# Base, expert and router weights in one product, lora a step later, and scores in two row tiles

## What is computed

```python
x = x + attn(cond(x))        # cond: a 32x32 mix of positions per sequence, with a bias
#   attn: q, k, v = x @ Wq, x @ Wk, x @ Wv; 32 query heads of 16, 8 kv heads, rope on q and k
#         scores = q k^T / 4, causal mask, softmax, times v, then @ Wo
x = x + ffn(cond2(x))        # cond2: a 9-tap grouped convolution along the 512, plus a context
#   ffn:  base_out = z @ base_W.T + base_b
#         probs = softmax(z @ router_W.T + router_b)      # 15 router outputs
#         w = the 8 largest probs, gathered per expert    # 8 experts
#         h = z @ A.T                                     # 8 experts x rank 16 = 128
#         lora = (h * w) @ B * 2
#         return base_out + lora
```

## Time and profile before

| | us |
|---|---|
| median of 3 runs | 747.89 (747.72 to 748.15) |
| the profiled execution | 748.08 |
| its span, first to last instruction | 746.1 |
| PE busy | 711.7 (95%) |
| DVE busy | 543.9 (73%) |
| ACT busy | 272.5 (37%) |
| POOL busy | 147.6 (20%) |
| chain that ended last: PE | 82% of the span |
| chain: ACT, POOL, DVE | 7%, 5%, 3% |
| granted TensorE clock, mean | 0.990 |

### The profile page before, as it was taken

The page is one execution under the profiler, slowest core; times in us unless marked ns, Lnnn a source line. Parts: engine busy times, 40 slices in busy tenths (PEclk is TensorE's granted clock), DMA queues, the critical chain, the costliest instruction groups (busy, mean ns, idle before and its releaser), DMA issues.

```text
span 746.1 us, 13077 instructions
## 1 busy us (share of the span) xinstructions
PE 711.7 (95%) x4478; PEld 628.5 (84%) x4510; DVE 543.9 (73%) x1424; ACT 272.5 (37%) x635; POOL 147.6 (20%) x116
## 2 busy tenths in 40 slices
PE   5879999999999999999999999999999999999985
PEld 4578888888888888888888888888889888888874
DVE  5457787777778777777877777788777777877763
ACT  4135433333443333344333323433333344333331
POOL 5232201222221122222102222210122222012211
PEclk9979999999999999999999999999999999999999
DMA  7751100111110011111100111110011111001000
GB/s 189 169 242 29 43 17 27 42 42 42 42 42 31 15 38 42 42 42 42 40 16 28 42 42 42 42 42 14 28 42 42 42 42 42 19 23 42 29 29 29
DMA packets 27392, 35.43 MB, mean 47 GB/s; under 512 B 11651, under 2 KB 13347, under 8 KB 26998
## 3 DMA queue, kind: packets, MB, share of 16 engines
q1 hardware_dynamic: 26374, 34.88, 15.1%
q10 hardware_dynamic: 864, 0.14, 0.1%
q0 software_dynamic: 144, 0.28, 0.1%
HBM read 26.36 MB, written 8.93 MB: 47 GB/s over the span
## 4 chain that ended last, share of the span: by engine, by line
PE 82%; ACT 7%; POOL 5%; DVE 3%; issue 2%; DMA 0%; POOLq 0%; SPq 0%; DVEq 0%
PE ps L375 37%; PE ps L516 11%; PE ps L545 11%; PE ps L528 8%; POOL z_lo L786 5%; ACT raw L644 4%; PE ps L552 2%; PE ps L579 2%; ACT z_hi L644 2%; PE ps L504 2%; PE ps L562 1%; PE ps L535 1%; PE ps L536 1%; PE ps L537 1%; PE ps L526 1%
## 5 line engine op out<-in xcount | busy, mean ns | idle before, releaser
L786 POOL TENSOR_TENSOR z_lo<-raw,z_hi 128x512 fp32r<-128x512 f32 x32 | 40.8, 1274 | 561.1 <-ACT z_hi L644 561.1
L545 PEld LDWEIGHTS ps<-convW,x1ph 128*128 128x128 f32 x768 | 90.6, 192 | 2.8
L545 PE MATMUL ps<-convW,x1ph 128*128 128x128 f32 x768 | 90.9, 275 | 0.0
L644 ACT ACTIVATE x1ph<-raw 32x128 f32<-32x128 f32 x256 | 78.9, 308 | 32.0 <-DVE raw L1016 29.4
L375 PE MATMUL ps<-wqkv_hi,y_hi 128*128 128x512 f32 (+1 forms) x256 | 90.5, 353 | 0.0
L375 PE MATMUL ps<-wqkv_hi,y_lo 128*128 128x512 f32 (+1 forms) x256 | 87.4, 341 | 0.0
L375 PE MATMUL ps<-wqkv_lo,y_hi 128*128 128x512 f32 (+1 forms) x256 | 87.3, 341 | 0.0
L644 ACT ACTIVATE qk_t<-ps 128x512 f32<-128x512 f32 x32 | 19.1, 598 | 177.5 <-PE ps L505 177.5
L811 DVE TENSOR_TENSOR oT_lo<-ps,oT_hi 128x512 fp32r<-128x512 f32 x32 | 22.1, 692 | 70.8 <-ACT oT_hi L644 70.8
L528 PE MATMUL ps<-qk_t 128*128 128x256 f32 x256 | 66.7, 383 | 4.4 <-issue 2.8
L723 ACT ACTIVATE raw<-raw 128x512 f32<-128x512 f32 x64 | 40.3, 630 | 76.5 <-DVE raw L985 76.5
(11 more groups left out here) (168 smaller groups left out, 1530.1 us busy)
## 6 DMA issues: line engine op xcount, KB each, us to landing
xm<-x SPq DMA_DIRECT2D x32, 256.0 KB, 2.6
xr<-x SPq DMA_DIRECT2D x32, 256.0 KB, 2.8
out<-raw SPq DMA_DIRECT2D x32, 256.0 KB, 2.0
convb<-convb_dram SPq DMA_DIRECT2D x1, 2048.0 KB, 12.2
mixb<-mixb_dram SPq DMA_DIRECT2D x1, 1792.0 KB, 8.7
raw<-L_attn_Wq SPq DMA_DIRECT2D x4, 256.0 KB, 4.0
raw<-L_attn_Wo SPq DMA_DIRECT2D x8, 128.0 KB, 4.5
raw<-L_ffn_base_W SPq DMA_DIRECT2D x1, 1024.0 KB, 5.8
```

What stands on the lines that cost most here:

```text
L545: last = mm(zo[:, :, b * S:(b + 1) * S], x1ph[:, b, s:s + P], convW[:, s, :, :], start=(s == 0), stop=(s == SHIFTS - 1))
L644: return nc.scalar.activation(dst, src, ACT.Copy)
L786: nc.gpsimd.tensor_tensor(z_lo[:, :, :].rearrange("p j n -> p (j n)"), zs, z_hi[:, :, :].rearrange("p j n -> p (j n)").bitcast(F32), ALU.s ...
```

## The change

The columns of base_W, A and router_W lie side by side in `ffn_hi` and `ffn_lo` (512 + 144 columns; the 256-column tile for A and router was padded, 143 columns are used, and one more pads them). One function `feed_forward` replaces `base` and `heads`: for each of the 12 pairs it issues a matmul of 384 columns (bank 6) and one of 272 (bank 7: the last 128 base columns and the 144). It is done in two halves, before and after `scores`. The last quarter of the output is summed in two parts: DVE adds bank 7 to x1b, and `lora` writes its last 128 columns to bank 5 by themselves.

`lora` moves one step later (t-3), and with it the output; there is one more step at the end (t up to 34). `qkv` is split in `queries` and `keys_values`, and `transpose_o` of the group before goes between them, into bank 4. `mix(t+1)` goes into bank 0 and stands before `conv`; it waits until the first half of softmax has read bank 0. `transpose_hw` goes last, into bank 1. `keys` masks over four kv heads: `kT` has 512 columns instead of 1024, and scores are eight matmuls with 64 rows (partitions 0 to 63 for h = 0, 64 to 127 for h = 1) and 128 columns, taken in turn from the two halves. The orders on ACT, DVE, POOL and SP follow.

```diff
+        ffn_hi = sb("ffn_hi", [P, PH, D + NAR], F32R)
+        ffn_lo = sb("ffn_lo", [P, PH, D + NAR], F32R)
+        base_hi, ar_hi = ffn_hi[:, :, 0:D], ffn_hi[:, :, D:D + NAR]
+        base_lo, ar_lo = ffn_lo[:, :, 0:D], ffn_lo[:, :, D:D + NAR]
...
-        qk_t = sb("qk_t", [P, D + NB * NKV * S])
+        qk_t = sb("qk_t", [P, TAPS * P])
         qT = qk_t[:, 0:D].rearrange("p (b g q) -> p b g q", b=NB, g=NQ)
-        kT = qk_t[:, D:].rearrange("p (b k m) -> p b k m", b=NB, k=NKV)
+        kT = qk_t[:, D:2 * D].rearrange("p (b k m) -> p b k m", b=NB, k=HK)
...
                     sp.dma_start(xr[:, :], group(x_g, t - 1)).then_inc(xr_in, 16)
-                if live(t - 2):
-                    wait(sp, out_sb, t - 1)
-                    sp.dma_start(group(out_g, t - 2), outS).then_inc(out_st, 16)
+                if live(t - 3):
+                    wait(sp, out_sb, t - 2)
...
-                wait(pe, out_sb, u - 2)
+                wait(pe, sx_sb, 2 * u - 1)
                 for c in range(KC):
-                    last = mm(ps[:, 6, c * P:(c + 1) * P], xm[:, c * P:(c + 1) * P],
+                    last = mm(ps[:, 0, c * P:(c + 1) * P], xm[:, c * P:(c + 1) * P],
...
-            def qkv(t):
+            def queries(t):
+
                 pe.wait_ge(y_hi_sb, t + 1)
...
+            def keys_values(t):
+
+                if live(t - 3):
+                    pe.wait_ge(hwT_hi_sb, t - 2)
+                    pe.wait_ge(hwT_lo_sb, t - 2)
...
+            def lora(u):
+
+                pe.wait_ge(hwT_hi_sb, u + 1)
+                pe.wait_ge(hwT_lo_sb, u + 1)
+                for n, (a, b) in enumerate(((hwT_hi, lora_hi), (hwT_hi, lora_lo), (hwT_lo, lora_hi))):
+                    mm(ps[:, 6, 0:BASE6], a[:, :], b[:, 0:BASE6], start=False, stop=(n == 2))
+                    last = mm(ps[:, 5, 0:P], a[:, :], b[:, BASE6:D], start=(n == 0), stop=(n == 2))
+                last.then_inc(ffn_ps, 1)
...
+            def feed_forward(u, phases):
+
+                for j in phases:
+                    for n, (a, b) in enumerate(((z_hi, ffn_hi), (z_hi, ffn_lo), (z_lo, ffn_hi))):
+                        first, final = j == 0 and n == 0, j == PH - 1 and n == 2
+                        mm(ps[:, 6, 0:BASE6], a[:, j, :], b[:, j, 0:BASE6], start=first, stop=False)
+                        last = mm(ps[:, 7, 0:P + NAR], a[:, j, :], b[:, j, BASE6:D + NAR], start=first, stop=final)
+                return last
...
                     mm(ps[:, h, :], ident16[:, :], causal16[:, :], start=True, stop=False)
-                    for b in (2 * h, 2 * h + 1):
-                        last = mm(ps[:, h, (b % 2) * 256:(b % 2) * 256 + 256], qT[:, b, :, :].rearrange("p g q -> p (g q)"),
-                                  kT[:, b, :, :].rearrange("p k m -> p (k m)"), start=False, stop=(b % 2 == 1))
-                    last.then_inc(s_ps, 1)
-
-            def lora(u):
-                pe.wait_ge(hwT_hi_sb, u + 1)
-                pe.wait_ge(hwT_lo_sb, u + 1)
-                mm(ps[:, 6, :], hwT_hi[:, :], lora_hi[:, :], start=False, stop=False)
-                mm(ps[:, 6, :], hwT_hi[:, :], lora_lo[:, :], start=False, stop=False)
-                mm(ps[:, 6, :], hwT_lo[:, :], lora_hi[:, :], start=False, stop=True).then_inc(ffn_ps, 1)
+                for b in range(NB):
+                    for h in range(2):
+                        rows = slice(h * P // 2, (h + 1) * P // 2)
+                        last = mm(ps[:, h, b * P:(b + 1) * P], qT[rows, b, :, :].rearrange("p g q -> p (g q)"),
+                                  kT[rows, b, :, :].rearrange("p k m -> p (k m)"), start=False, stop=(b == NB - 1))
+                        if b == NB - 1:
+                            last.then_inc(s_ps, 1)
...
+                wait(pe, x1_sb, t)
...
+            def transpose_hw(u):
+
+                pe.wait_ge(hw_sb, u + 1)
+                nc.tensor.transpose(ps[:, 1, 0:P], hw[:, :, :].rearrange("p e r -> p (e r)"), ident).then_inc(hwT_ps, 1)
...
+            def transpose_o(u):
+
+                pe.wait_ge(on_sb, u + 1)
                 for b in range(NB):
-                    last = nc.tensor.transpose(ps[:, 6, b * P:(b + 1) * P], on[:, b, :], ident)
+                    last = nc.tensor.transpose(ps[:, 4, b * P:(b + 1) * P], on[:, b, :], ident)
                 last.then_inc(oT_ps, 1)
...
             def steps(t):
                 if live(t):
-                    qkv(t)
+                    queries(t)
+                if live(t - 1):
+                    transpose_o(t - 1)
+                if live(t):
+                    keys_values(t)
...
+                if live(t - 3):
+                    lora(t - 3)
...
+                if peeled(t, 2):
+                    pe.wait_ge(base_lo_sb, PH)
                 if live(t - 2):
-                    base(t - 2)
-                    transpose_hw(t - 2)
+                    pe.wait_ge(z_hi_sb, t - 1)
+                    pe.wait_ge(z_lo_sb, t - 1)
+                    wait(pe, out_sb, t - 2)
+                    feed_forward(t - 2, (0, 1))
                 if live(t):
                     scores(t)
                 if peeled(t, 1):
                     prepare_base((2, 3))
                 if live(t - 2):
...
+                    feed_forward(t - 2, (2, 3)).then_inc(ar_ps, 1)
...
                 if live(t + 1):
                     mix(t + 1)
                 if peeled(t, -1):
                     mixing_weights()
+                if live(t - 1):
+                    conv(t - 1)
+                if live(t):
+                    transpose_p(t)
+                if peeled(t, 0):
+                    pe.wait_ge(prep_sb, 2)
                 if live(t):
                     values(t)
...
+                if live(t - 2):
+                    transpose_hw(t - 2)
```

ACT, POOL and DVE:

```diff
-                    for h in range(2):
+                for h in range(2):
+                    if live(t):
                         act.wait_ge(sx_sb, 2 * t + 1 + h)
...
+                    if h == 0 and live(t - 2):
+                        act.wait_ge(ar_ps, t - 1)
+                        copy(arS[:, :], ps[:, 7, P:P + NAR]).then_inc(ar_sb, 1)
+                if live(t + 1):
+                    act.wait_ge(ys_sb, t + 2)
+                    copy(y_hi[:, :], ys[:, :]).then_inc(y_hi_sb, 1)
...
+                if live(t - 2):
+                    act.wait_ge(lgs_sb, t - 1)
+                    nc.scalar.activation(ex[:, :], lgs[:, :], ACT.Exp).then_inc(ex_sb, 1)
...
+                if live(t - 2):
+                    pool.wait_ge(x1_sb, t - 1)
+                    pool.wait_ge(ld["basebB"], 16)
+
+                    wait(pool, out_sb, t - 2)
+                    nc.gpsimd.tensor_tensor(x1b, x1, basebB[:, :].rearrange("p (n j) -> p j n", j=PH),
+                                            ALU.add).then_inc(x1b_sb, 1)
...
+                    pool.wait_ge(zs_sb, t)
+                    pool.wait_ge(z_hi_sb, t)
+                    nc.gpsimd.tensor_tensor(z_lo[:, :, :].rearrange("p j n -> p (j n)"), zs,
+                                            z_hi[:, :, :].rearrange("p j n -> p (j n)").bitcast(F32),
+                                            ALU.subtract).then_inc(z_lo_sb, 1)
...
-                                kvmask.unsqueeze(1).unsqueeze(3).broadcast_to([P, NB, NKV, S]), ALU.mult).then_inc(kT_sb, 1)
+                                ps[:, 3, 0:P].rearrange("p (b m) -> p b m", m=S).unsqueeze(2).broadcast_to([P, NB, HK, S]),
+                                kvmask.unsqueeze(1).unsqueeze(3).broadcast_to([P, NB, HK, S]), ALU.mult).then_inc(kT_sb, 1)
...
+                if live(t - 3):
+                    dve.wait_ge(hwT_hi_sb, t - 2)
+                    minus(hwT_lo[:, :], ps[:, 1, 0:P], hwT_hi[:, :]).then_inc(hwT_lo_sb, 1)
+                if live(t):
+                    rope(t, 0, q_ps, 0, D)
                 if live(t - 1):
                     dve.wait_ge(oT_ps, t)
                     dve.wait_ge(oT_hi_sb, t)
...
+                if live(t):
+                    rope(t, 1, qkv_ps, D, P)
+                    roped(t)
+                if live(t - 3):
+                    dve.wait_ge(ffn_ps, t - 2)
+                    dve.wait_ge(last_sb, t - 2)
+
+                    wait(dve, out_st, 16 * (t - 3))
+                    out3 = outS.rearrange("p (n j) -> p j n", j=PH)
+                    v.tensor_tensor(out3[:, 0:3, :], ps[:, 6, 0:BASE6].rearrange("p (j n) -> p j n", j=3), x1b[:, 0:3, :], ALU.add)
+                    v.tensor_tensor(out3[:, 3, :], ps[:, 5, 0:P], x1b[:, 3, :], ALU.add).then_inc(out_sb, 1)
+                if live(t):
+                    keys(t)
                 if live(t - 1):
                     dve.wait_ge(wo_ps, t)
...
                     softmax(t)
...
+                if peeled(t, 0):
+                    prepare_lora()
+                    prepare_ar()
+                    prepare_conv()
+                    prepare_experts()
+                if peeled(t, 1):
+                    prepare_base((2, 3))
```

(62 more changed lines are left out.)

118 lines of the change are left out of this document (34 added, 84 removed).

## The result

The changed kernel takes 802.98 us (median; 798.44 to 808.54) against 747.95 before (747.72 to 748.15): a ratio of 1.074, 95% interval 1.067 to 1.081. It is slower by 55 us, where 14 us less were forecast, and outside the range.

A forecast was written before the change was run, and what follows sets the result against it. PE was taken as the bound, with 0.27 us of slack. Steps falling from 21.63 to 21.16 give -14.1 over 30 steps, head -4.9, tail +4.4: -14.6 in all, so 733.5 us, range 721 to 750.

The forecast's parts named there:

- Scores: PE's scores as eight half-row matmuls: 1.55 us with overlapping tiles and most of both passages, between bounds 1.33 and 2.54.
- the passages: Changes between full and half tiles around scores: each may empty the array, 0.16 us each, 0.32 in all, mostly counted.
- B: Rival at scores: tiles don't overlap but change without cost; scores 2.22, step 21.48, time 743.1; chance 0.18.
- C: Rival at scores: no overlap and both passages empty the array; step 21.80, time 752.7, slower; chance 0.17.
- Stall of values: Before values on PE: nothing covers ACT's copy prT any more, a stall of 0.49 us in every step.
- mix held by DVE: Before mix on PE: DVE's softmax subtraction ends at 14.03, so mix stalls 0.35 us and runs at 14.26.
- hw's transpose: Last PE piece of a step: put in the step sum at 0.11 us, with no wait.
- The clock: In the head's idle time: keeping the granted clock up might give 1.7 us, losing it costs as much.
- Head: Start of the run: second queries go before the first group's transpose_o and y_lo comes earlier, -4.9 us.
- Tail: End of the run: later last feed forward, bank 7 sum, lora and output-sum wait, less earlier conv: +4.4 us.
- Rival E: DVE's list is longer than laid out (output sum 1.5, x1b contending with keys): +0.4 us a step; chance 0.07.

The follow-up runs named there:

- experiment 1: The changed kernel with one added wait: POOL starts z_lo only after DVE's hw of the same step; 744.97 us, against 748.38 before on that chip.
- experiment 3: The changed kernel with hw's transpose moved behind the next step's queries, into bank 7; 741.15 us, timed again 740.24, ratio 0.986 to the kernel before.
- experiment 9: The kernel with hw's transpose behind the next queries, with DVE's first-step preparations, including the twelve convW copies, put back ahead of ys; 741.11 us, ratio 0.990.
- after: The changed kernel as first measured, with no follow-up edit, against the kernel before: 802.98 us, ratio 1.074.
- experiment 6: The changed kernel with DVE's routing up to hw (route2) moved ahead of zs, POOL untouched; 773.82 us.
- experiment 7: The kernel with hw's transpose behind the next queries, with conv, mix and transpose_p before feed forward's last quarter, DVE reordered, filling transposes in the last steps; 758.97 us.

## Why the prediction was wrong

*The bound before* was read rightly: PE. In experiments 1 and 3, where only the stall of values is left, the step is 21.23 and 21.12 against the 21.16 forecast. PE in experiment 1, which has PE's order of the change, and DVE:

```profile
388.95 0.47 PE L377 MATMUL ps<-wqkv_hi,y_hi 128*128 128x512 f32 x1
...
400.17 1.16 PE L544 MATMUL ps<-qk_t 64*128 64x128 f32 x16
401.26 0.45 PE L529 MATMUL ps<-ffn_hi,z_hi 128*128 128x384 f32 x1
...
403.18 1.13 PE L472 MATMUL ps<-mixw,xm 128*128 x8
...
402.31 0.69 DVE L1004 TENSOR_TENSOR raw<-ps,mx 128x512 f32<-128x512 f32 x1
```

The terms of the sum, one by one:

- *Scores*, 1.55 forecast: the tiles overlap. In experiment 1 the masks take 0.54 up to the tiles (400.17 - 399.63), the sixteen instructions 1.09 to the next matmul, and that one is at 0.29 instead of 0.18: 1.74. Single instructions of the trace show how: the two halves start in pairs 0.007 apart, and from the second pair on the pairs follow at 0.11, the pace at which conv's full-row matmuls follow one by one. At that pace eight pairs are the 0.90 forecast. What was mis-sized is the passages: 0.11 before the tiles, 0.10 behind the first pair, 0.09 behind the last, 0.11 behind the next matmul, together 0.41 where I had put in 0.22. Rivals B and C fall: the serial cost would have been 2.22 or more.
- *Stall of values*, 0.49: right; from transpose_p's start to values it is 406.12 - 404.83 = 1.29 in experiment 3 (1.36 forecast).
- *mix held by DVE*, 0.35: didn't happen, and yet mix came when forecast. In experiment 1 the queries start at 388.95; DVE's subtraction ends 14.05 later (402.31 + 0.69; 14.03 forecast) and mix starts 14.23 later (14.26 forecast), but it doesn't wait: PE's own work up to it takes these 14.23, and not 13.91. Of the 0.32 more, 0.19 is scores and 0.12 feed forward; the smaller differences of the other pieces cancel. So the hit of the sum (21.16) is partly luck: a wait put in that wasn't there made up for work that was priced too low.
- *hw's transpose, 0.11 and no wait: this is the step that failed.* I laid out DVE's list up to mix and stopped there. Behind it stand ys, zs and the routing, and this time hw's transpose hangs on them at the very end of PE's step, so that the late hw went straight onto the path: +1.05 a step, 28 us over the 27 steps from 4 to 31. Of all the rows of before I took durations as if they belonged to the instruction, when this one depends on what POOL does meanwhile.
- *The clock.* I gave it 1.7 us either way in the head and nothing in the steps, though the earlier trace rows shows what idle time does to it. Three stops of 1.1 us together cost 1.54 more in most steps. On the mean of the steps it is 23.56 - 22.28 = 1.28, times 27 = 34 us, more than the waits that set it off. With the -0.40 x 27 = -11 that the change brings without both, it is the 52 us of these steps.
- *Head*, -4.9: -3.2 up to group 1. Its queries do start early, at 38.97 (43 forecast), but transpose_o waits 4.85 behind them. Group 1's own step then gives back 1.9 (76.51 - 53.08 = 23.43 against 21.57 before), since it has no feed forward yet, so that PE comes early to mix and waits 2.5 for DVE's softmax. I had moved the twelve copies behind ys at their old 1.81; but experiment 9, with the copies at 1.80, has the same wait of 2.5 and no shorter head.
- *Tail*, +4.4: +6.3, and +7.1 in experiment 3. The last two hw waits are 3.1 each there, and the clock is at 0.50 behind the first: the last feed forward starts at the lower clock.

```profile
718.64 0.47 PE L578 MATMUL ps<-cst,hw 128*128 128x128 f32 x1 [3.07 <-DVE hw L959]
...
722.96 0.66 PE L526 MATMUL ps<-ffn_hi,z_hi 128*128 128x384 f32 x1 [1.24 <-DVE raw L1034]
...
720.00:725.00 5.00, 3.76 (x13) 3.49 (x14) 1.06 (x2) 0.00 (x0) 1.55 (x1) 0.50 0.14 52
```

Experiment 3 has -1.3 (54.90 - 56.24), -12.9 and +7.1 in the three columns of the first table: it lacks 3.6 in the head, 1.2 in the steps (2.3 in group 1's, as in after, of which the others give back about half) and 2.7 in the tail, and that is why the repaired kernel ends at 740 and not at 733.5. Rival E named the right engine with a wrong place (DVE before mix, not after), and at +0.4 a step, with no clock, a price six times too small.

What stays open: what decides whether the clock falls in a given step (five steps of after with the same stops kept it, and one stop of 1.19 in experiment 6 lowered it in 8 of 27 steps; single stops of 0.25, and of 0.28 and 0.41 some 7 us apart in experiment 7, never did in these steps); and how the tail's loss divides between clock and waits, since no run had a tail without stops.

## What to carry to other kernels

Lay out every engine's list to the end of the step, not only up to the first join, and ask of the last instruction of the step on the bound engine what it waits for: move it behind work that doesn't need it (here, from the end of the step to behind the next queries, some 60 us less). Before taking a vector duration from a trace, look at what GpSimd ran beside it, before and after the reordering. And price short stops of TensorE twice: for themselves, and for a fall of the clock behind them.

## What the runs showed of the hardware

- Two operations of VectorE with two SBUF inputs were held until an operation of GpSimd ended: hw took 0.35 alone and 1.42 beside z_lo (ending 0.15 behind it), sel 0.17 alone and 0.58 beside y_lo (ending 0.02 behind it). The reduction and the reciprocal beside y_lo kept their 0.17 and 0.16. The Trainium skill states this (SBUF — State Buffer, "Who interferes with whom"): the pair of ports that the two engines share is an exclusive lock, and a VectorE instruction with one SBUF input or none, outside the modes that use both ports, doesn't contend. The runs agree.
- The twelve 32x32 copies went from 1.81 to 7.30 beside wo_lo. The same section of the Trainium skill counts copies among what can take both ports. That POOL caused it here is argued from this, and from POOL being idle in the runs with 1.81 and 1.80; no run changed POOL alone.
- TensorE fell to 1.2 GHz (granted clock 0.50) behind three stops of 0.25, 0.56 and 0.28 us in otherwise steady work, in 22 of 27 steps of after; in the step shown the pitch is near 0.23 again from 422.54. With the first two filled it didn't fall in any of them. One stop of 1.19 lowered it in 8 of 27 steps (experiment 6).
- After a wait at the end of the loop's body the next matmul came 0.61 us behind the transpose (418.84 - 418.23), 0.56 with the gap filled and 0.22 where the transpose hadn't waited. After the same wait of 0.56 outside the loop, in the last such step of after, it was 0.33 (746.40 - 746.07), so most of it belongs to the loop's end. It is not shown what this is; it costs 0.3 to 0.4 beside the wait itself.
- Two row tiles with 64 rows, 128 columns each, taken in turn, start in pairs 0.007 us apart with 0.11 from pair to pair, against 0.112 for one full-row matmul of that width in conv: two for the time of one. With the passages sixteen take 1.09. A weight load of 64 rows takes no less than one of 128 (0.188 and 0.192 in the trace), so the gain comes from the overlap. By TensorEngine Tiling (Array Packing), Key Properties, in the Trainium skill the tiles load and multiply in parallel and a change of mode drains the array; the first can be seen here, and each of the two changes costs about 0.2 us.
